# Whole stack rows, a ring of four residual images, and a new order of the steps in a fused conv and window-attention kernel

## What is computed

```
x = x + L0(groupnorm32(x))     # router: softmax of mean and std per image picks 2 of 8 experts
                               # shared 1x1 grouped conv + 2 expert 3x3 grouped convs,
                               # each: group norm over 16 channels, affine, SiLU; weighted sum
x = x + L1(groupnorm32(x))     # q, k, v = 1x1 conv; 8x8 windows, 8 heads of 16, softmax(qk/4 + bias) v
                               # plus a 7x7 depthwise conv of v; then a 1x1 projection
```

## Time and profile before

| | us |
|---|---|
| median of three runs | 871.91 |
| the profiled execution | 872.17 |
| its span, first to last instruction | 870.4 |
| PE busy | 674.7 (78%) |
| DVE busy | 601.1 (69%) |
| ACT busy | 450.8 (52%) |
| POOL busy | 185.9 (21%) |
| mean granted TensorE clock | 0.894 |
| DMA moved | 145.29 MB, 167 GB/s |

### The profile page before, as it was taken

The page is one execution under the profiler, slowest core; times in us unless marked ns, Lnnn a source line. Parts: engine busy times, 40 slices in busy tenths (PEclk is TensorE's granted clock), DMA queues, the critical chain, the costliest instruction groups (busy, mean ns, idle before and its releaser), DMA issues.

```text
span 870.4 us, 18688 instructions
## 1 busy us (share of the span) xinstructions
PE 674.7 (78%) x6926; PEld 409.1 (47%) x6926; DVE 601.1 (69%) x1136; ACT 450.8 (52%) x746; POOL 185.9 (21%) x289
## 2 busy tenths in 40 slices
PE   5225829696979788797979697979796969788785
PEld 4212315464646454555545454646463647444321
DVE  4734456778778787869687777777777888532396
ACT  1114445565657474746565556656565655354321
POOL 3122042222223130404130312222221011000044
PEclk9987759697989898989989897979797979999999
DMA  8232553948575664759594939394956345587345
GB/s 344 105 120 67 178 149 94 197 120 203 131 188 152 168 191 142 189 156 192 142 208 137 219 102 220 110 215 123 209 128 167 108 130 156 183 275 248 121 183 203
DMA packets 92751, 145.29 MB, mean 167 GB/s; under 512 B 24691, under 2 KB 65782, under 8 KB 92662
## 3 DMA queue, kind: packets, MB, share of 16 engines
q1 hardware_dynamic: 66806, 100.90, 41.1%
q0 software_dynamic: 21248, 25.36, 14.3%
q10 hardware_dynamic: 4608, 17.86, 5.6%
HBM read 84.21 MB, written 51.41 MB: 156 GB/s over the span
## 4 chain that ended last, share of the span: by engine, by line
PE 50%; DVE 20%; issue 12%; DMA 11%; ACT 3%; POOL 2%; POOLq 1%; SPq 1%; DVEq 0%; ACTq 0%
PE g L1069 14%; PE g L1087 5%; PE g L1065 5%; PE pv L1152 4%; PE t L1137 4%; DVE xr L840 4%; PE s L1126 3%; DMA vt<-x 3%; PE s L1259 3%; DMA xs<-xn 3%; PE g L1170 2%; PE t L1259 2%; PE g L1097 2%; PE s L1122 2%; DMA xsh<-xs 2%
## 5 line engine op out<-in xcount | busy, mean ns | idle before, releaser
L525 ACT ACTIVATE y<-g 128x512 f32<-128x512 f32 x96 | 57.1, 597 | 192.2 <-PE g L1065 104.4
L1069 PE MATMUL g<-xsh,wsel 96*128 96x512 f32 x256 | 132.1, 645 | 16.1 <-DMA xsh<-xs 15.4
L810 DVE BATCH_NORM_STATS2 st<-y 128x6 f32<-128x512 f32 x96 | 66.3, 692 | 99.1 <-ACT y L525 99.1
L874 DVE TENSOR_REDUCE mx<-s 128x8 f32<-128x512 f32 x128 | 87.2, 681 | 28.6 <-PE s L1126 27.9
L878 DVE TENSOR_TENSOR less<-s,mx 128x512 f32<-128x512 f32 x128 | 88.5, 692 | 4.4
L1122 PE MATMUL s<-bias,ident 128*128 128x512 f16 x128 | 51.1, 399 | 51.7 <-DMA stack<-sk_d 51.7
L1137 PE MATMUL t<-ident,less 128*128 128x128 f32 x512 | 79.4, 278 | 15.1 <-ACT pt L596 15.1
L596 ACT ACTIVATE pt<-t 128x512 f32<-128x512 f32 x128 | 74.7, 596 | 24.6 <-PE t L1137 18.0
L1137 PEld LDWEIGHTS t<-ident,less 128*128 128x128 f32 x512 | 62.4, 145 | 49.8 <-issue 36.9
L1152 PE MATMUL pv<-vp,pt 128*64 128x34 f32 x2048 | 82.8, 227 | 3.0 <-DVE ot L892 2.6
L1069 PEld LDWEIGHTS g<-xsh,wsel 96*128 96x128 f32 x256 | 49.5, 207 | 72.8 <-issue 54.0
(11 more groups left out here) (159 smaller groups left out, 1176.5 us busy)
## 6 DMA issues: line engine op xcount, KB each, us to landing
xsh<-xs POOLq DMA_DIRECT2D x64, 210.0 KB, 7.3
stack<-sq_d SPq DMA_DIRECT2D x96, 128.0 KB, 5.2
stack<-sk_d SPq DMA_DIRECT2D x192, 64.0 KB, 5.2
xs<-xn ACTq DMA_DIRECT2D x16, 578.0 KB, 3.3
vt<-x SPq DMA_DIRECT2D x4, 2048.0 KB, 18.3
xin<-x POOLq DMA_DIRECT2D x16, 512.0 KB, 7.8
acc_d<-xr SPq DMA_DIRECT2D x16, 512.0 KB, 5.1
sq_d<-qhl SPq DMA_DIRECT2D x32, 256.0 KB, 2.1
```

The source lines that it names most:

```text
L525: act.activation(y[:, k, h * HALF:(h + 1) * HALF], g[at][:, :], ACT.Identity).then_inc(g_free[at], 1)
L810: last = v.bn_stats(st[:, 2 * k + h, :], y[:, k, h * HALF:(h + 1) * HALF])
L874: v.tensor_reduce(mx[:, p % 2, :], scored, AX.X, ALU.max).then_inc(sem["s_max"], 1)
L1069: last = mm(g[at][:, :], wsel[:, k - 1, C * dy:C * dy + C], xsh[:, k - 1, dy + 16 * h:dy + 16 * h + 16, 0:W], start=(dy == 0), stop=(dy == 1))
```

## The change

The q and k projections are computed with their output channels in another order (`order` in `_lay_out`), so that the four channels that share a partition row of the stack lie in consecutive rows of `sq_d` and `sk_d`. Both are laid out by half. A stack row of a half is then 4 KB in one run, and a half is loaded by 4 DMAs for q and 4 for k. `xr` becomes a ring of four images, `x1` and the save and reload between them go; only the images 0 to 11 are saved for the end, the last four stay. k half h is projected in the slot of q half h. The average of x moves behind the convolutions of slot 6. Several pieces change their slot on DVE, ACT, POOL and SP.

```diff
@@ bank_uses
-        use("y2", b + 2, (0,))
-        use("q", b + 1, (0,))
-        use("y2", b + 2, (1,))
-        use("q", b + 1, (1,))
-        use("k", b + 1)
+        for h in range(2):
+            use("y2", b + 2, (h,))
+            use("q", b + 1, (h,))
+            use("k", b + 1, (h,))
@@ tiles
-        xr = sb("xr", [C, PIX])
-        x1 = sb("x1", [C, PIX])
+        xr = sb("xr", [C, KEEP, PIX])
-        sq_d = nc.dram_tensor("sq_d", [2, C, PIX], F16).ap()
-        sk_d = nc.dram_tensor("sk_d", [2, C, PIX], F16).ap()
-        acc_d = nc.dram_tensor("acc_d", [B, C, PIX], F32).ap()
+        sq_d = nc.dram_tensor("sq_d", [2, 2, C, HALF], F16).ap()
+        sk_d = nc.dram_tensor("sk_d", [2, 2, C, HALF], F16).ap()
+        acc_d = nc.dram_tensor("acc_d", [B - KEEP, C, PIX], F32).ap()
@@ SP
+            def save_qk(j):
                 for half in range(2):
                     save_half(j, half, "q", sq_d, qhl, q_saved)
                     save_half(j, half, "k", sk_d, khl, k_saved)
+            def high_rows(src, half, a):
+                return src[half, 0].rearrange("(a c i) n -> a c (i n)", a=2, i=Q)[a]
+            def both_rows(src, half, a):
+                size = C * HALF
+                return bass.AP(src.tensor, 2 * half * size + a * size // 2, [[size, 2], [Q * HALF, HD], [1, Q * HALF]])
             def stack_q(j, half):
...
-                for part, t in enumerate((0, 1, 0)):
-                    sp.dma_start(qs[QD * part:QD * part + QD, :, cols],
-                                 sq_d[t, :, cols].rearrange("(i c) n -> c i n", i=Q)).then_inc(stacked[half], 16)
+                for a in range(2):
+                    dst = qs[3 * HD * a:3 * HD * (a + 1), half, :, :].rearrange("p i n -> p (i n)")
+                    sp.dma_start(dst[0:HD], high_rows(sq_d, half, a)).then_inc(stacked[half], 16)
+                    sp.dma_start(dst[HD:3 * HD], both_rows(sq_d, half, a)).then_inc(stacked[half], 16)
             def stack_k(j, half):
...
-                for part, t in enumerate((0, 0, 1)):
-                    for par in range(2):
-                        rows = QD * part + HD * par
-                        src = sk_d[t, :, cols].rearrange("(i a c) n -> a c i n", i=Q, a=2)
-                        sp.dma_start(ks[rows:rows + HD, :, par, cols], src[par]).then_inc(stacked[half], 16)
+                for a in range(2):
+                    dst = ks[3 * HD * a:3 * HD * (a + 1), half, a, :, :].rearrange("p i n -> p (i n)")
+                    sp.dma_start(dst[0:2 * HD], both_rows(sk_d, half, a)).then_inc(stacked[half], 16)
+                    sp.dma_start(dst[2 * HD:3 * HD], high_rows(sk_d, half, a)).then_inc(stacked[half], 16)
-            (save_xr and load_x1 go)
             def step(b, has1, has2, has3):
-                if b: load_x1(b - 1)
-                if has1: save_q(b + 1); save_k(b + 1); stack_q(b + 1, 0); stack_k(b + 1, 0)
-                if b: save_acc(b - 1)
-                if has1: stack_q(b + 1, 1); stack_k(b + 1, 1); place_v(b + 1)
-                if has2: save_xr(b + 2)
+                if has1: save_qk(b + 1); stack_k(b + 1, 0); stack_q(b + 1, 0)
+                place_v(b)
+                if 0 < b <= B - KEEP: save_acc(b - 1)
+                if has1: stack_k(b + 1, 1); stack_q(b + 1, 1)
@@ POOL step: split_v(b + 1) goes behind load_x(b + 4) and rsqrt(b + 2, 1, 1)
@@ ACT step
+                    if p != 5 or not has1: exponential(b, p)
+                    if has3 and p == 0: normalise(b + 3)      # was behind copy_y and high_qk
                     if p < 2: copy_y(b + 2, 2, (p,)); high_qk(b + 1, 0, p); high_qk(b + 1, 1, p)
                     if p == 5 and has1:
-                        vt_out(b + 1)
+                        vt_out(b + 1, 0); exponential(b, p); vt_out(b + 1, 1)
@@ ACT, taps
-                    act.wait_ge(sem["acc_saved"], 16 * B)
+                    act.wait_ge(sem["acc_saved"], 16 * (B - KEEP)), and pr of the last image emptied
@@ DVE
             residual(j, 0):
-                        dve.wait_ge(sem["xr_saved"], 16 * j)
-                        dve.wait_ge(sem["xw_done"], j)
+                    if j >= KEEP:
+                        dve.wait_ge(sem["acc_saved"], 16 * (j - KEEP + 1))
             step: low_qk(b + 1, 1, p) in slots 0 and 1 (both were in slot 2)
                   y_coefs(b + 2) in slot 3 ahead of outputs, x_coefs(b + 2) in slot 7 behind maxima
                   residual(b + 2, 0) in slot 4 (all three parts were in slot 5)
                   y_stats(b + 3, 0) ahead of group_variance(b + 2, 1, 1) in slot 6
                   turn_v(b + 1) in slot 7 (was in slot 4, ahead of residual)
@@ PE step
                     if p < 2: convolve(b + 2, 2, (p,)); project_qk(b + 1, 0, p); project_qk(b + 1, 1, p)
                     if p == 6:
-                        average(b + 2, 1, 1, AV4)
                         convolve(b + 3, 0)
                         convolve(b + 3, 1, (0,))
+                        average(b + 2, 1, 1, AV4)
```

More of the change, by code:

```diff
@@ L193, in program @@
         ri = sb("ri", [B, 8], U32)
-        l1s = sb("l1s", [3, C])
+        l1s = vn[0:3, 0:C]
         hb = o[:, 0:TABLE]
-        free = [y[:, n, :] for n in range(3)] + [xin[:, 0, :], xin[:, 1, :], xr[:, :], x1[:, :], xw[:, :], o[:, :]]
+        free = [y[:, n, :] for n in range(3)] + [xin[:, 0, :], xin[:, 1, :], xw[:, :], o[:, :]]
         free += [t[:, :, :].rearrange("p t n -> p (t n)").bitcast(F32) for t in (qhl, khl)]
@@ L201, in program @@
         free += [vp_flat[:, n * PIX:(n + 1) * PIX] for n in range(4)]
-        acc = free[0:B]
+        acc = free[0:B - KEEP] + [xr[:, n, :] for n in range(KEEP)]
         evac = [stack[:, n * PIX:(n + 1) * PIX] for n in range(2)]
@@ L600, in step @@
                 for p in range(PAIRS):
-                    exponential(b, p)
+                    if p != 5 or not has1:
+                        exponential(b, p)
+                    if has3 and p == 0:
+                        normalise(b + 3)
                     if p < 2:
@@ L606, in step @@
                             high_qk(b + 1, 0, p)
-                        if has3 and p == 0:
-                            normalise(b + 3)
-                    if p == 2 and has1:
-                        high_qk(b + 1, 1, 0)
-                        high_qk(b + 1, 1, 1)
+                            high_qk(b + 1, 1, p)
                     if p == 3:
@@ L620, in step @@
                     if p == 5 and has1:
-                        vt_out(b + 1)
+                        vt_out(b + 1, 0)
+                        exponential(b, p)
+                        vt_out(b + 1, 1)
                     if p == 6 and has3:
@@ L668, in _ @@
                 if c == 1:
-                    act.wait_ge(sem["acc_saved"], 16 * B)
-                if c:
+                    act.wait_ge(sem["acc_saved"], 16 * (B - KEEP))
+                    for h in range(2):
+                        wait_emptied(act, "pr", B - 1, h)
+                if 0 < c <= B - KEEP:
                     load_acc(c - 1)
@@ L938, in step @@
                             low_qk(b + 1, 0, p)
[L939 to L943 removed]
+                            low_qk(b + 1, 1, p)
                     if p == 4:
@@ L947, in step @@
                             add_projection(b - 1, 1)
+                        if has2:
+                            residual(b + 2, 0)
+                    if p == 5 and has2:
+                        residual(b + 2, 1)
+                        residual(b + 2, 2)
+                    if p == 6:
+                        if has3:
+                            y_stats(b + 3, 0)
+                        if has2:
+                            group_variance(b + 2, 1, 1)
+                    if p == 7:
+                        if has3:
+                            y_stats(b + 3, 1)
                         if has1:
                             turn_v(b + 1)
-                    if p == 5 and has2:
-                        for part in range(3):
-                            residual(b + 2, part)
-                    if p == 6:
-                        if has2:
-                            group_variance(b + 2, 1, 1)
-                        if has3:
-                            y_stats(b + 3, 0)
-                    if p == 7 and has3:
-                        y_stats(b + 3, 1)
             for k in range(3):
```

129 lines of the change are left out of this document (50 added, 79 removed).

## The result

| | before | after |
|---|---|---|
| median, us | 871.82 (4 runs) | 923.45 (920.66 to 926.71, 4 runs) |
| ratio, 95% interval | | 1.059 [1.054, 1.064] |
| the profiled execution | 872.17 | 920.66 |
| 13 steps, first residual sum of image 2 to that of 15 | 541.02, 41.62 each | 586.23, 45.09 each |
| the rest | 331.15 | 334.43 |

Each ratio leaves out the runs that were over 1.5% slower than the kernel's fastest: one of e1, one of e9 and one of e14 (in both of these the profiled one) and two of the four of e15.

A forecast was written before the change was run, and what follows sets the result against it. A chain through PE with holes was taken to bound the step: 13 x (41.62 - 37.0) = 60.1 us gained; 872.2 - 60.1 - 2.6 + 2.5 - 1.0 = 811 us. The range was 776 to 846 us.

The forecast's parts named there:

- The failed step: Stack half 0: issue at 8.1 us, 11.0 on two engines, 3 for shifted rows and x; step grows 2.0 to 37.0 us.
- The clock: Shared convolution on PE: its four matmuls lose 1.8 us at granted clock 0.50; that loss was left out of the new step.
- the forecast's own case: `both_rows` on two engines, half 0 landing 3.3 us after PE wants it: 37.0 us a step, 811 us, chance 63%.
- The second rival: PE's waits in slot 6 bring the clock to 0.50 again: 39.8 us a step, 847 us, chance 12%.
- The step without late transfers: 31.9 us of PE's own work plus 3.1 us of remaining waits: 35.0 us a step.
- The average: Average of x behind slot 6's convolutions: its 2.89 us wait on PE goes, cost 0.14 us.
- What could be late next: Root, coefficients and window, some 4 us from the average to the first q projection, covered by 7 us of PE work.
- The residual sum: First residual sum on DVE: 1.22 us instead of 2.65, as POOL no longer splits v under it.
- DVE: 30.9 us of DVE work in a 35.0 us step, with gaps only in waits for PE or ACT.
- Around the steps: Outside the 13 steps: step 13 gains 2.6 us, step 15 loses 2.5, prologue gains 1.0, tail nothing.
- The rival "spread": Stack loads spread over all engines, stack early: 35.0 us a step, 783 us, chance 16%.
- The rival "two engines saturate": Two engines need longer than a step for 812 KB: 908 us at 18.3 GB/s, 944 at 17.2; chance 8%, slower.

The follow-up runs named there:

- e1: The changed kernel with the `both_rows` stack loads at a slow dimension of sixteen instead of two (16 engines); 789.06 us, 0.907 of the kernel before.
- e9: The changed kernel with the shifted rows' slow dimension the sixteen channels instead of the three shifts; 891.32 us, 1.020 of the kernel before.
- e14: e9 with half 0 of the stack asked for between the saves of half 0 and half 1; 865.16 us, 0.992 of the kernel before.
- e15: e1 with v evacuated in one piece behind the exponential of slot 5, as before the change; 792.84 us, no ratio.
- e13: e9 with v and the saved residual issued behind half 1 of the stack; 888.35 us, 1.018 of the kernel before.
- e7: The changed kernel with v and the saved residual issued behind half 1 of the stack; 908.21 us, 1.045 of the kernel before.
- e8: e1 with v and the saved residual issued behind half 1 of the stack; 786.07 us, 0.904 of the kernel before.
- e10: e8 with the shifted rows at a slow dimension of sixteen too; 777.64 us, 0.892 of the kernel before.
- e11: e1 with the average of x back ahead of the convolutions of slot 6; 832.18 us, 0.953 of the kernel before.
- e12: e1 with `turn_v` back in slot 4 and POOL's split of v ahead of the load of x; 816.15 us, 0.938 of the kernel before.

## Why the forecast failed, step by step

- **The failed step** is "8.1 + 11.0 + 3 is 22.1 us, 3.3 us after PE wants it", and in it the length of the transfer. The transposes of slot 1 start at 367.6 in the step shown, so the first issue is 7.4 us behind them instead of 8.1 and PE asks at 19.3 instead of 18.8; the count of engines and their rate were right. The transfer took 19.1 us in the step shown and 18.3 to 25.4 over the twelve, 20.6 on average, not 14.0. The shifted rows are worth 2.4 us of it (e9: 18.2 us), near the 2.9 that the forecast had in its 3 us; v and the residual, which it had put at nothing, 0.6 to 1.2 (e13, e7). With both out of the way e13 still takes 17.6 us from first issue to arrival, against 11.0 of bytes. This remainder of 6.6 us is what the sum lacked. By estimate, at 25.1 GB/s: 512 KB of saves just ahead, 1.3 us on each engine; the load of x that crosses, 1.3 us (the forecast had "a share of x" in its 3); and a save of 256 KB, 0.65 us of bytes, takes 2.3 us to land, so 1.7 us pass otherwise. Some 2 us more are not located.
- **The clock** was put at nothing in the forecast's own case, and that failed too. There PE stood 4.3 us and kept its clock; in the real one it stood 6.5 to 13.6 us for the stack, and in the step shown the clock costs 2.1 us. A wait as short as the forecast's would not have kept it either: behind stands of 1.7 to 3.2 us in e14 the shared convolution takes 3.0 to 3.5 us instead of 2.17. The second rival had this, at 12%.
- **The step without late transfers**, 35.0 us: measured 35.02 in e1, e8 and e10. The parts were less good than the sum: waits of 0.80, 0.76 and 0.32 us (e10) where I had 1.0, 1.2 and 0.6 (and 0.3 for small ones), hence 33.1 us of PE's own work and not 31.9. Two errors of 1.2 us cancel; that the sum came out is luck.
- **The average** behind the convolutions: no wait, 0.14 us from its start to the next transposes (401.24 to 401.38). Right, and worth 3.2 us a step (e11). What could be late next, the window behind it, was seen as well; it is covered here, and in e12 it is not.
- **The residual sum** at 1.22 us: right. All sixteen in the changed kernel:

```profile
L819 DVE TENSOR_TENSOR xr<-y,xin x16: 1215/1216/1226, 78.9 to 743.0; 128x1024 f32<-128x1024 f32 x16
```

- **DVE** in a quiet step: 30.1 us, forecast 30.9. No row shows a cost of the ring, of the shared slots of q and k or of the added waits.
- **Around the steps**: 1.1 us gained in the forecast, 3.3 lost. From the first sum of image 15 on it is 177.7 us (920.66 - 742.99) against 174.4 before, so the loss lies there. PE waits for the stack three times more after that sum, 3.20, 4.19 and 2.61 us, 10.0 in all where 2.5 were forecast; e1 has no such wait and 169.3 us.
- **The rival "spread"** gave 783 us; e1 has 789. As a forecast of this kernel 16% was not too low, for the loads were not spread; as a change it would have been the thing to do first.
- **The rival "two engines saturate"** had the sign and at 8% too little of the chance, and its mechanism is not what happened: its rate was 17.2 to 18.3 GB/s an engine, and 27 were measured; e14 has steps of 40.6 us on average with the bytes on the two engines that e9 has, and in the changed kernel both stand idle at the end of the 12 us shown above. The engines have time enough over a step; between the first issue and PE's demand they have not. The forecast priced the deadline once, at 14.0 us of transfer, and gave no chance to 19.

## What to carry to other kernels

Before a DMA gets longer rows, look at the slow dimension of its pattern: swapping two dimensions here was worth 134 us, longer rows by themselves 0 to 2.5%. Price a transfer on few engines at its deadline, with everything that is queued ahead of it there, and take the whole time from first issue to landing from a row, since bytes over rate gave 11 us of 18. Price the clock behind a wait with the wait. And a transfer on few engines can slow the well-spread ones behind it (e14).

## What the runs showed of the hardware that was not expected

- A save of 256 KB landed after 18.4 us instead of 2.3 when it was issued behind loads that keep two engines busy (e14).
- With the shift as the slow dimension the 64 loads of shifted rows made 13,312 packets more (21248 against 7936 in POOL's queue, the same megabytes), 208 a load, and landed in 5.4 us instead of 3.7 (e9).
- The granted clock fell to 0.50 behind stands of 2.6 us (e11) and 7.2 us (changed kernel), behind one of 0.66 us it did not (e1). It can fall after PE has started again: behind a stand of 2.65 us the first matmul took 0.39 us, as at full clock, and the convolution 1.5 us later 3.24 us instead of 2.17 (e14).
